# A redrawn order for all five engines in a three-layer graph network, with four staging buffers for the first weights

## The reference: what is computed

```python
h = jnp.maximum(_layernorm(x, axis=-1), 0.0)
for l in range(3):
    si = x @ attn_w[l, :d];  sj = x @ attn_w[l, d:]
    scores = si[:, :, None] + sj[:, None, :] + attn_b[l]
    scores = jnp.where(scores >= 0, scores, 0.2 * scores)
    scores = jnp.where(mask, scores, -jnp.inf)          # mask = adj + eye > 0
    agg = jnp.einsum('bij,bjd->bid', softmax(scores), x)
    h = layernorm(x + agg, g1[l], beta1[l])
    ff = gelu(h @ W1[l] + b1[l]) @ W2[l] + b2[l]         # hidden width 1024
    x = layernorm(h + ff, g2[l], beta2[l])
return x_input + x
```

## Time and profile before

| | before |
|---|---|
| median of 3 runs (lowest, highest) | 1359.9 us (1359.55, 1360.2) |
| the profiled execution, its own time | 1360.92 us |
| its span, first to last instruction | 1359.1 us |
| mean granted TensorE clock | 0.987 |
| PE busy / PEld busy | 1267.5 us (93%) / 1133.0 us (83%) |
| DVE / ACT / POOL busy | 1128.7 us (83%) / 924.8 us (68%) / 658.0 us (48%) |

### The profile page before, as it was taken

One profiled execution on the slowest core, in us unless ns is written; L12 is line 12 of the kernel. 1 busy time (PEld: TensorE's weight loads), 2 busy tenths in 40 slices (PEclk: granted clock), 3 DMA queues, 4 the chain that ended last, 5 costly groups with the idle time before them and its releaser, 6 DMA issues.

```text
span 1359.1 us, 23270 instructions
## 1 busy us (share of the span) xinstructions
PE 1267.5 (93%) x8065; PEld 1133.0 (83%) x8065; DVE 1128.7 (83%) x3325; ACT 924.8 (68%) x1754; POOL 658.0 (48%) x538
## 2 busy tenths in 40 slices
PE   0599999999999999999999999999999999999994
PEld 0388888888888898988888898998888898989983
DVE  4778788889997888889898878879998888888773
ACT  3476766677776677677777776777777677677751
POOL 1235434553565355345545543553565445445454
PEclk9699999999999999999999999999999999999997
DMA  6100001001221000001121100000121100000012
GB/s 205 62 17 17 16 32 40 0 1 41 69 61 50 1 1 1 1 1 32 55 63 32 40 1 1 1 1 3 58 80 41 32 1 1 1 1 1 1 32 78
DMA packets 39265, 39.91 MB, mean 29 GB/s; under 512 B 1736, under 2 KB 37612, under 8 KB 39148
## 3 DMA queue, kind: packets, MB, share of 16 engines
q1 hardware_dynamic: 39148, 38.43, 8.9%
HBM read 30.04 MB, written 8.39 MB: 28 GB/s over the span
## 4 chain that ended last, share of the span: by engine, by line
PE 59%; DVE 26%; POOL 7%; issue 4%; DMA 2%; ACT 1%; SPq 0%; POOLq 0%; DVEq 0%
PE acc L700 28%; PE hbank L685 23%; DVE xs L536 7%; POOL rstd L332 3%; PE util L735 3%; DVE hid_lo L435 3%; PE acc L715 3%; DVE st L454 3%; DVE xs L523 2%; PE util L742 2%; DVE mv L415 2%; DVE st L422 1%; DMA hb<-in_x_dram 1%; DVE st L530 1%; POOL xout L375 1%
## 5 line engine op out<-in xcount | busy, mean ns | idle before, releaser
L700 PE MATMUL acc<-w2hi,hid_hi 128*128 128x256 f32 x1536 | 441.4, 287 | 0.0
L700 PE MATMUL acc<-w2hi,hid_lo 128*128 128x256 f32 x1536 | 434.3, 283 | 0.0
L700 PE MATMUL acc<-w2lo,hid_hi 128*128 128x256 f32 x1536 | 434.1, 283 | 0.0
L332 POOL TENSOR_TENSOR rstd<-ve,halfs 128x4 f32<-128x4 f32 x112 | 122.7, 1095 | 598.2 <-DVE ve L417 598.0
L595 ACT ACTIVATE hbank<-hbank,vec 128x512 f32<-128x512 f32 x384 | 254.6, 663 | 188.2 <-PE hbank L685 184.9
L685 PE MATMUL hbank<-ht_hi,w1hi 128*128 128x512 f32 x768 | 320.2, 417 | 2.5 <-DVE hid_lo L435 2.5
L685 PE MATMUL hbank<-ht_lo,w1hi 128*128 128x512 f32 x768 | 302.6, 394 | 0.0
L685 PE MATMUL hbank<-ht_hi,w1lo 128*128 128x512 f32 x768 | 301.2, 392 | 0.0
L435 DVE TENSOR_TENSOR hid_lo<-hbank,hid_hi 128x512 fp32r<-128x512 f32 x384 | 258.8, 684 | 46.3 <-ACT hid_hi L601 46.3
L700 PEld LDWEIGHTS acc<-w2lo,hid_hi 128*128 128x128 f32 x1536 | 293.7, 191 | 4.0
L700 PEld LDWEIGHTS acc<-w2hi,hid_hi 128*128 128x128 f32 x1536 | 293.3, 191 | 4.0
(11 more groups left out here) (62 smaller groups left out, 1750.1 us busy)
## 6 DMA issues: line engine op xcount, KB each, us to landing
xres<-in_x_dram SPq DMA_DIRECT2D x16, 512.0 KB, 4.0
out_dram<-xout SPq DMA_DIRECT2D x32, 256.0 KB, 2.3
xraw<-in_x_dram SPq DMA_DIRECT2D x14, 512.0 KB, 3.7
xout<-in_L_gnn_W_dram SPq DMA_DIRECT2D x12, 512.0 KB, 3.9
adji<-in_adj_dram SPq DMA_DIRECT2D x16, 256.0 KB, 2.9
hb<-in_x_dram SPq DMA_DIRECT2D x2, 512.0 KB, 9.6
attn_rows<-in_L_gnn_attn_w_dram SPq DMA_DIRECT2D x1, 768.0 KB, 5.7
ln_rows<-in_L_gnn_g_dram SPq DMA_DIRECT2D x2, 384.0 KB, 7.4
```

Source lines behind the costliest of these rows:

```text
L332: pool.tensor_tensor(rstd[n][:], ve[n][:], halfs[:], ALU.pow).then_inc(rstd_n[n], 1)
L700: mm = pe.matmul(to, v[:, k % HID, of_g], w[:, i.l, c], start=c == 0 and n == 0 and g % HG == 0, stop=c == C - 1 and n == 2, skip_group_ch ...
```

## The change

`sj_rows` stays on PE. The edits outside the orders, with the loads ahead of SP's first slot:

```diff
-diag = sb("diag", [P, P])
+diag = sb("diag", [P, P], BF16)
-b2_rows = xres[:, 0:L]
+b2_rows = xs[:, 1, 0:L]
-w_in = [sem(f"w_in{i}") for i in range(2)]
+w_in = [sem(f"w_in{i}") for i in range(4)]
...
-def half_staged(n, w):
-    t = xout[:, n % 2]
+def half_staged(n):
+    t = (xout[:, 0], xout[:, 1], xs[:, 2], xres[:])[n if n < 4 else n % 2]
+def half_arrived(n):
+    return (w_in[n], 16) if n < 4 else (w_in[n % 2], 16 * (n // 2))
...
 def load_weights(n):
-        wait(sp, w_lo, n - 1)
+        if n >= 4:
+            sp.wait_ge(w_lo, n - 1 if n >= 6 else n - 3)
...
 def slot(s):                       # SP
+        if 4 <= s + 5 < len(halves):
+            load_weights(s + 5)
...
-    for s in range(-4, ITEMS + 2):
+    load_xraw(item(0))
+    load_small()
+    load_adj(item(0))
+    load_xraw(item(1))
+    load_b2_rows()
+    load_weights(0)
+    load_weights(1)
+    load_ln1_rows()
+    load_xraw(item(2))
+    load_weights(2)
+    load_weights(3)
+    load_ln2_rows()
+    for s in range(-6, ITEMS + 3):
...
 def h_gamma(i, h):
-        pool.wait_ge(z1_n, GG * i.q + HG * (h + 1))
+        pool.wait_ge(z1_n, GG * (i.q + 1) if h else GG * i.q + HG)
...
 def residual(i, h):
-            else:
-                dve.wait_ge(w_lo, len(halves))
...
 def h_out(i, m):
+        if i.q == 0 and m == 0:
+            act.wait_ge(vec_ready, 1)
...
 def first_x(i):
+        if i.q == 1:
+            act.wait_ge(ln1_ready, 1)
+        if i.q == 2:
+            act.wait_ge(w_lo, 3)
```

More of the change, by code:

```diff
@@ L548, in slot @@
                     dve.tensor_copy(vec[:], util[:, 0:NV]).then_inc(vec_ready, 1)
[L549 to L552, removed]
+                if t:
+                    low(t, 7)
+                if a:
+                    j_dots(a)
+                if f:
+                    h_low(f, 1)
+                if d and d.l == 0:
+                    input_shift(d)
+                if a:
+                    i_dots(a)
+                    add_bias(a)
@@ L553, in slot @@
+                if t:
+                    residual(t, 0)
+                    residual(t, 1)
+                    moments2(t)
+                if b:
+                    attend(b, 0)
+                if f:
+                    low(f, 0)
+                if t:
+                    norm2(t, 0)
+                if b:
+                    attend(b, 1)
+                if f:
+                    low(f, 1)
+                if b:
+                    moments1(b)
                 if f:
                     low(f, 2)
-                    low(f, 3)
@@ L556, in slot @@
[L556 to L572, removed]
@@ L573, in slot @@
-                if p and p.l == 0: input_shift(p)
-                if b: low(b, 0)
-                if f:
[L576 to L581, removed]
+                if t:
+                    norm2(t, 1)
+                if a and a.l == 0:
+                    penalty(a)
+                if f:
+                    low(f, 3)
+                if a:
+                    masked(a)
@@ L582, in _ @@
+                if b:
+                    norm1(b)
+                if f:
+                    low(f, 4)
+                if p and p.l == 0:
+                    input_moments(p)
+                if a:
+                    minus_max(a)
+                if f:
+                    low(f, 5)
+                    low(f, 6)
+                split_weights(s + 4)
+                if b:
+                    h_low(b, 0)
+            for s in range(-6, ITEMS + 3):
                 slot(s)
@@ L586, in _, with round_weights @@
         def _(act):
[L587 to L590, removed]
+            def round_weights(n):
+                if 0 <= n < len(halves):
+                    act.wait_ge(*half_arrived(n))
+                    act.copy(half_on_chip(0, *halves[n]), half_staged(n)).then_inc(w_hi, 1)
             def gelu(i, c):
@@ L643, in slot @@
             def slot(s):
[L644 to L647, removed]
+                t, f, b, a, d = item(s - 1), item(s), item(s + 1), item(s + 2), item(s + 3)
+                if t:
+                    gelu_high(t, 7)
                 if f:
+                    h_high(f, 1)
+                if b:
+                    exps(b)
+                    et_out(b)
+                if f:
+                    gelu_high(f, 0)
+                    gelu_high(f, 1)
+                if d and d.l == 0:
+                    first_x(d)
+                round_weights(s + 4)
+                if f:
+                    gelu_high(f, 2)
                     gelu_high(f, 3)
                     gelu_high(f, 4)
[L651 to L660, removed]
+                if a:
+                    leaky(a)
+                if f:
+                    gelu_high(f, 5)
+                    gelu_high(f, 6)
                 if b:
[L662 to L665 removed]
+                    h_high(b, 0)
+            for s in range(-6, ITEMS + 3):
                 slot(s)
@@ L763, in slot @@
                     ffn2(f, 6)
[L764 to L769, removed]
+                    ffn2(f, 7)
+                if b:
+                    ffn1(b, 0)
+                if a:
+                    e_turn(a)
+                if b:
+                    ffn1(b, 1)
                 if a:
@@ L772, in slot @@
                     aggregate(a, 1)
-            for s in range(-4, ITEMS + 1):
+                if b:
+                    ffn1(b, 2)
+                    ffn2(b, 0)
+                    ffn1(b, 3)
+                    ffn2(b, 1)
+                    ffn1(b, 4)
+                if d:
+                    sj_rows(d)
+                if b:
+                    ffn1(b, 5)
+                    ffn1(b, 6)
+                    ffn2(b, 2)
+            for s in range(-6, ITEMS + 3):
                 slot(s)
```

112 lines of the change are left out of this document (43 added, 69 removed).

## The result

The changed kernel takes 1327.93 us (median; 1327.76 to 1328.97) against 1359.82 us for the kernel before (medians of four executions each): ratio 0.9767, 95% interval 0.9750 to 0.9784. The forecast was 1322.4 with a range of 1314 to 1335. The profiled execution took 1327.76 us, with a span of 1326.0, against 1359.1 before.

A forecast was written before the change was run, and what follows sets the result against it. PE was taken as the bound, with 30.5 us of waits, partly for DVE's late norm1. Head 59.0 + 46 periods 1197.4 + last two items 48.2 + tail 15.5 + tight places 1.5 = 1321.6 span; median 1322.4 us, range 1314 to 1335.

The forecast's parts named there:

- rival 1: Layer 0's lead-in: late xraw load, then variance meeting x_beta, delay z1_turn's second half 1.1 us; +6.6, 1329 us; chance 0.13.
- tight places: Allowance of 1.5 us in all for places where work lands only just in front of PE.
- Head: Start of the kernel until the first ffn1, in the frame of a period: 59.0 us, range 50 to 62.
- three steps in a row: Head: first weight half at about 14.9, POOL's row add at about 19.7, rstd of item 0 at 22.6 us.
- Period: One steady item on PE, same pieces in the new order: 26.03 us in place of 26.09.
- hand-laid frame: One period laid out by hand: everything lands in front of PE by 0.3 to 1.1 us.
- second lag: Layer 0's lead-in: the raw input's variance may meet x_beta on POOL and lose 1.3 us.
- Tail: After the last matmul: 15.5 us in place of 20.0, the last add no longer waiting for xres.
- rival 5: h_gamma's new threshold equals the old one in both halves, so that edit has no effect; no separate chance.
- Rival 2: DVE stays the bound around layers 2 and 0, 12.5 us of waits remain: 1334 us; chance 0.07.
- Rival 3: Two-input DVE instructions, penalty and splits, also wait for POOL: about +11 us, 1333 us; chance 0.10.
- Rival 4: x_gamma slips beside norm1 again, PE loses about 1.0 us per item: 1369 us; chance 0.04 whole, 0.04 in part.

The follow-up runs named there:

- experiment 2: Changed kernel with POOL making item 0's rstd before its wait for the row loads; 1323.78 us, ratio 0.9732.
- experiment 1: Changed kernel with SP loading adj and xraw one item earlier, ahead of the wait for penalty; 1320.16 us, ratio 0.9708.
- experiment 3: Changed kernel with two weight staging buffers again in place of four; 1327.88 us, ratio 0.9762.
- Experiment 5: Kernel before, with one edit: both halves of h_gamma wait for all four instructions of norm1; 1344.71 us, ratio 0.9885.
- experiments 7 and 8: 7: changed kernel with four spare row statistics on DVE ahead of norm1, 1359.3 us, ratio 0.9995; 8: see experiment 8.
- experiments 4 and 10: Both h_gamma halves wait for all of norm1; 4: on the changed kernel, 1329.72 us; 10: on it with earlier adj and xraw and new head, 1314.41 us.
- experiment 8: Changed kernel with POOL's second x_gamma held until norm1's first instruction is done, so it runs beside norm1; 1348.16 us, ratio 0.9903.

## Why the prediction was right, and where it was not

The steady period, the head and the tail came as forecast, and rival 1 came with them: 1327.93 is 5.5 us above the forecast's 1322.4 and 1.1 below rival 1's 1329, to which I had given 0.13. That it still lies in the forecast's own range (1315 to 1328) is luck: that width was meant for the head and for 0 to 3 us of tight places, and without the 1.2 us that the head came out shorter it would have been passed. By the terms of the sum:

- **Head**, 59.0 predicted, 57.84 measured (83.89 - 26.05). The three steps in a row happened: the first half was taken at 14.84 (14.9 predicted), the row add ran at 18.32 (about 19.7), nmr could start at 21.13 (22.6). The row loads came 1.4 us sooner than the distances of the earlier trace rows gave; experiment 2 shows that they were the chain. input_moments(3) did wait for its load, as predicted.
- **Period**, 26.03 predicted, 26.05 in this execution, 26.03 in that of experiment 1 and both in that of experiment 3. The pieces of the earlier trace rows did add up (there are 22 calls per item on PE, not 28; the pieces are the eight of ffn1, eight of ffn2, four turns and aggregate's two).
- **The reading of the old steady stretch was wrong.** I called 26.09 PE's own floor and put 3 us of gain on a better sequence of pieces. Experiment 5 shows 26.01 for the old sequence. The new one is no cheaper, and the 3 us came from a wait for norm1 that PE's rows do not show and those of its weight loads do (experiment 5). The sum was right because it was made of new pieces, not of that difference.
- **Nothing holds PE in the steady period**: right. The margins of 0.3 to 1.1 us of the hand-laid frame were real: 0.92 and 0.68 by the trace, about 0.6 by experiments 7 and 8.
- **Layer 0's lead-in** is the term that was mis-sized. The 1.5 us allowed for tight places measured 6.2. The step that failed was xraw "lands about 16.4": it was issued at 12.8 (12.4 in the prediction) but input_moments could start at 17.9, 5.2 us after the issue, where I had allowed 4. With 4.0 it would have been 16.8, 0.4 behind low(X,4). Rival 1 had 1.1 us for six items, +6.6. Its second lag, the variance meeting x_beta, was not needed in items 10 and 11; in the other four it came too and made the variance 0.1 (items 22 and 23), 0.3 (35) and 0.5 us (34) later than the load alone. "It needs two small lags at once" was the wrong reason to give it 0.13: the first lag brings the second, since a late variance starts behind x_beta's start.
- **Tail**, 15.5 predicted, 15.56 measured, and the last two items 48.28 for 48.2.
- **h_gamma's threshold**: rival 5 holds for this edit, the numbers are equal and h_gamma still starts after half of norm1. A true wait for the whole norm is worth 15.5 us in the old order (experiment 5) and nothing in the new one (experiments 4 and 10). In the old order norm1 was late; in the new one x_gamma no longer meets it, and it has 0.6 us to spare.
- **Rival 2** is out: experiment 1 has DVE doing the same work and no wait. **Rival 3** is out as to its price: penalty took 0.68 beside x_gamma (item 10 above). The splits, which it named too, did get longer, 1.31 for 1.22, and made POOL's next instruction 2.31 long, but no period of items 1 to 8, where they stand, grew by it:

```profile
126.92 1.31 POOL L359 TENSOR_TENSOR hb<-hb,ln_rows 128x512 f32<-128x512 f32 x1
128.00 1.31 DVE L421 TENSOR_TENSOR w2lo<-xout,w2hi 128x1024 fp32r<-128x1024 f32 x1
```

The rule it rested on (the Trainium skill, "GPSIMD Engine Reference", Key points) is now borne out by pairs that the kernel before never ran, these splits and j_dots, which both read two operands from SBUF: j_dots took 1.51 beside an add on POOL of 1.44, and 0.42 otherwise. For penalty it depends on which starts first: penalty had started 0.16 earlier, and here POOL's instruction took 1.67 for 1.28. In the changed kernel these hits land where DVE has time: they stand in experiment 1 too, where no item is long.
- **Rival 4** would have needed 0.8 us per item to decide, and has about 0.4 by experiment 8.

In sum: 1321.6 - 1.2 (head) + 0.9 (pace) + 6.2 - 1.5 (lead-in) + 0.1 (the end) is 1326.1, and the span was 1326.0. The last 1.1 us are in the step from span to median: I took 1.0 off for the median, which lay 0.2 above the profiled run here.

Of the 33.1 us, then, norm1's contention was the largest single part: one line removes 15.5 in the old order, and bringing it back into the new one costs 16 to 20 (experiment 8). The rest of the new order removes a further 10.5 in items 1 to 45 (1188.8 to 1178.3), 1.1 ahead of item 1, 1.6 in the last two and 4.4 after them. These are differences between kernels, not effects tried one by one, but for the lines named above; which of the moved calls gives the 10.5 is not shown.

## What to carry to other kernels

Take an instruction's start to the next one's start, piece by piece, before calling a fully busy stretch a floor, and test it by removing the suspected wait: here 0.08 us per item, and up to 0.4, hid under "busy". Ask for the waits of PE's weight loads as well as for those of its matmuls. When an order is tightened, list each queue in which a load stands behind a wait for a consumer: SP's adj-then-xraw order cost 7.8 us here. And a contended instruction is worth its length only while it is late: the same line gave 15.5 us in one order and nothing in the other.

## What the runs showed of the hardware

- Four kinds of DVE instruction were held by POOL here. Started while a POOL tensor instruction runs, each ends behind POOL's end by its own length less 0.14 to 0.26 us: the variance's last one (0.17 alone) by 0.03, norm1's (0.40) by 0.15, j_dots (0.42) by 0.28, split_weights (1.22) by 1.08. So j_dots took 1.51 beside a POOL instruction of 1.44, and 2.02 beside one of 1.86. j_dots or penalty that started first, by 0.05 us or more, kept its length, and POOL's grew (1.28 to 1.67). A lead of less than 0.01 us was not enough: norm1's first instruction in the earlier trace rows started that little ahead of x_gamma and took 1.44.
- PE's busy time does not see waits shorter than the shown length of a matmul. In experiment 8 PE is busy 1191.71 of 1194.41 us, while the 45 items take 22 us more than 45 x 26.05: only 2.7 of the 22 are seen. The waits of the weight loads show more of it, there 7.3 us for norm1 and 8.1 for low.
- The same PE program runs at 26.03 or 26.05 per item, from one execution to the next (experiment 1 against the changed kernel) and within one (experiment 2: 26.03 up to item 9, 26.05 from item 12 on, at full clock). Most of the 0.02 is in one piece, ffn1 behind aggregate, 1.58 against 1.56.
